# Layer 0 attention: DVE's copy and maximum stand ahead of the next pair's query piece in a step, not behind it

## The reference, cut to what matters

```python
q_lat = rmsnorm(hidden_states @ q_a_w, q_a_norm_w)
q = (q_lat @ q_b_w).reshape(b, s, H, QKD).transpose(0, 2, 1, 3)
...
q_pe = rope_interleaved(q_pe, pos)
scores = (jnp.einsum('bhqd,bhkd->bhqk', q_nope, k_nope) + jnp.einsum('bhqd,bhkd->bhqk', q_pe, k_pe)) * QKD ** (-0.5)
...
scores = jnp.where(mask[:, None], scores, -jnp.inf)
attn = jax.nn.softmax(scores, axis=-1)
out = jnp.einsum('bhqk,bhkd->bqhd', attn, v).reshape(b, s, H * VD)
```

## Time and profile before

| | |
|---|---|
| median of 3 runs | 1736.12 us (1732.72 to 1740.18) |
| the profiled execution | 1737.15 us, its span 1735.4 us |
| layer 0 attention in it | from about 520 to 1115 us |
| busy, share of the span | PE 94%, DVE 62%, ACT 49%, POOL 41% |
| mean granted clock of PE | 0.986 of full |

### The profile page before, as it was taken

One profiled execution on the slowest core, in us unless ns is written; L12 is line 12 of the kernel. 1 busy time (PEld: TensorE's weight loads), 2 busy tenths in 40 slices (PEclk: granted clock), 3 DMA queues, 4 the chain that ended last, 5 costly groups with the idle time before them and its releaser, 6 DMA issues. The chain is left out here.

```text
span 1735.4 us, 27207 instructions
## 1 busy us (share of the span) xinstructions
PE 1631.3 (94%) x8810; PEld 1220.1 (70%) x8810; DVE 1080.6 (62%) x2489; ACT 847.6 (49%) x1591; POOL 716.8 (41%) x740
## 2 busy tenths in 40 slices
PE   6899998999988999999999999899989999999998
PEld 5688887788776766776677777587755555568887
DVE  3556657999838767777777777435776776510222
ACT  3456555443326555555555555444245565653321
POOL 1212213444657656666556666376201111322221
PEclk9999999999999999999999999999989999999999
DMA  8522223221100000000000000373432332231111
GB/s 243 171 76 90 91 77 93 60 63 34 55 31 7 25 19 19 31 19 20 25 19 19 31 19 13 92 236 122 151 62 50 84 66 61 51 103 55 49 49 49
DMA packets 113020, 114.16 MB, mean 66 GB/s; under 512 B 39776, under 2 KB 72000, under 8 KB 112896
## 3 DMA queue, kind: packets, MB, share of 16 engines
q1 hardware_dynamic: 110592, 108.40, 21.9%
q10 hardware_dynamic: 2304, 4.20, 0.7%
HBM read 83.97 MB, written 28.44 MB: 65 GB/s over the span
## 5 line engine op out<-in xcount | busy, mean ns | idle before, releaser
L1463 ACT ACTIVATE a_p<-a_sm,a_nmax 128x640 f32<-128x640 f32 (+7 forms) x256 | 198.7, 778 | 142.6 <-DVE a_nmax L1424 140.9
L1506 POOL TENSOR_SCALAR a_p<-a_p,a_rinv 128x640 f32<-128x640 f32 (+7 forms) x256 | 191.9, 753 | 165.0 <-DVE a_rinv L1432 162.1
L1424 DVE CUSTOM_DVE_ANT_0 a_sm<-ps,maskb 128x640 f32<-128x640 f32 (+7 forms) x256 | 192.0, 750 | 98.4 <-PE ps L1368 96.5
L2360 DVE CUSTOM_DVE_ANT_0 ga_sm<-ps,strip 128x640 f32<-128x640 f32 (+1 forms) x224 | 163.1, 754 | 71.2 <-PE ps L2267 69.7
L2381 ACT ACTIVATE ga_pt<-ps 128x1024 f32<-128x1024 f32 (+1 forms) x192 | 147.9, 810 | 112.7 <-PE ps L2290 111.7
L1380 PE MATMUL ps<-ident,a_p 128*128 128x128 f32 x1152 | 172.4, 275 | 14.0 <-DVE a_pt L1439 13.8
L1380 PEld LDWEIGHTS ps<-ident,a_p 128*128 128x128 f32 x1152 | 135.3, 140 | 39.7 <-issue 16.9
L2421 POOL TENSOR_SCALAR_AFFINE_SELECT ga_pt<-ga_pt 128x512 f32<-128x512 f32 x64 | 40.7, 636 | 265.1 <-ACT ga_pt L2381 265.0
L1368 PE MATMUL ps<-kh,lq_qh 128*128 128x512 f32 (+4 forms) x384 | 128.8, 389 | 18.4 <-DVE a_nmax L1424 11.6
L940 DVE SCALAR_TENSOR_TENSOR idx<-ix_r,ix_sgc,idx 128x256 f32<-128x256 f32 (+6 forms) x105 | 90.7, 884 | 73.9 <-ACT ix_r L905 73.9
L1395 PE MATMUL ps<-a_pt,vst 128*64 128x512 f32 (+3 forms) x768 | 134.2, 492 | 1.9 <-DVE a_pt L1439 1.1
(11 more groups left out here) (313 smaller groups left out, 3979.2 us busy)
## 6 DMA issues: line engine op xcount, KB each, us to landing
idx<-ctx_d SPq DMA_DIRECT2D x32, 256.0 KB, 3.3
idx<-wvo_d SPq DMA_DIRECT2D x32, 256.0 KB, 3.8
ga_qst<-qkd SPq DMA_DIRECT2D x42, 128.0 KB, 4.2
f_wr<-in_L_ffn_w SPq DMA_DIRECT2D x18, 256.0 KB, 2.8
x<-in_L_attn_hidden_states SPq DMA_DIRECT2D x16, 256.0 KB, 4.3
op_wo<-in_L_attn_o_w SPq DMA_DIRECT2D x8, 512.0 KB, 5.0
ix_w<-in_L_attn_idx_wq_w SPq DMA_DIRECT2D x64, 64.0 KB, 1.9
ix_fo<-in_L_attn_o_w SPq DMA_DIRECT2D x8, 512.0 KB, 4.1
```

The lines of the kernel that those rows point to most:

```text
L1424: dve.tensor_tensor_reduce(out=in_row(sm[kind][:, 0:w], w), in0=in_banks(slots[kind], w), in1=in_row(maskb[:, MASK_OFF[t]:MASK_OFF[t + 1]] ...
L1463: act.activation(p[kind][:, v // 2 % 2, 0:w], sm[kind][:, 0:w], ACT.Exp, bias=nmax[:, v % 4:v % 4 + 1], scale=-1.0, accum_out=rsum[:, v % ...
L1506: pool.tensor_scalar(mine, mine, rinv[:, v % 4:v % 4 + 1], 1.0, ALU.mult, ALU.mult).then_inc(norm_done, 1)
L2360: dve.tensor_tensor_reduce(out=in_row(sm[kind][:, 0:w], w), in0=in_banks(slots[kind], w), in1=in_row(strip[:, S - w:], w), scale=-1.0, sca ...
```

## The change

In DVE's step, `dve_hook` moves from behind the inverse to the end. In steps 3, 5, 8 and 11 (and -5 and -3 of the lead-in), DVE so copies the transposed blocks of unit `u+2` and takes the maximum of unit `u+7` first and turns the piece of queries after that. In all other steps the hook is empty and nothing changes. The programs of the other engines, all semaphores and all their counts stay the same.

```diff
@@ -1442,11 +1442,11 @@
                 def step(i, u, left):
                     if there(u + 5, left):
                         inverse(i, u + 5)
-                    q["dve"](dve, i, u, left)
                     if there(u + 2, left):
                         keep(i, u + 2)
                     if there(u + 7, left):
                         maximum(i, u + 7)
+                    q["dve"](dve, i, u, left)
```

## The result

| | before | after |
|---|---|---|
| median | 1736.32 us (6 runs) | 1804.11 us (6 runs, 1801.61 to 1812.39) |
| ratio | | 1.0396, interval 1.0376 to 1.0415 |
| the profiled execution, span | 1735.4 us | 1801.5 us |
| mean granted clock of PE | 0.986 | 0.981 |

The forecast was 1794 us, with 1765 to 1812 around it. The page after, against the earlier trace rows; the instruction counts are the same.

The account below looks back on a forecast made before the run. PE was taken to bound the kernel, busy 94% of the span. Costs of 3.96 us in each of 14 pairs plus 2.7 in pair 0 sum to 58.1 us, giving 1794 us against the median, range 1765 to 1812.

Parts of the forecast that it names:

- First cost: Step 3: piece 0 waits behind unit 10's maximum, so PE's product for piece 1 gets its bank 1.45 us later.
- Second cost: Step 5: piece 1 waits behind unit 12's maximum, delaying POOL's low half; unit 16's scores 3.74 us later, including 1.45 from step 3.
- Steps 9 to 14: From unit 16's scores to step 14: DVE stalls go, POOL's queue takes their place, 0.22 us lost a pair.
- most of the 0.74 us a pair that PE waits for copies is gone: Sign of being right: PE's transposes mostly stop waiting for DVE's copies out of the transpose banks.
- The sum: 3.96 us a pair over pairs 1 to 14 (55.4), 2.7 in pair 0, lead-in 0: 58.1 us in all.
- The lead-in: Before pair 0: the 2.31 us stop goes but unit 8 waits for piece 3; taken as 0, bounds -2.3 and +1.
- The clock: PE's new stops of about 1.5 us each were taken to cost 0 beyond themselves, by the lead-in's 2.31 us stop.
- Rival (c): PE's clock also falls behind the new stops, 1 to 2 us a pair: 1815 us; chance 0.05.
- (a): Rival: PE waited for copies and maxima, and the pieces have slack; 18 us come back, 1718 us; chance 0.06.
- (b): Rival: one cost only; just the bank wait, 1758 us, or just the second cost, 1771 us; chance 0.12.
- (d): Rival: the effects cancel or DVE's order shows nowhere, 1733 to 1740 us; chance 0.05.
- The gain: At most all of PE's two DVE stalls, for copies and maxima: 1.21 us a pair, 18 us over 15 pairs.

Follow-up runs that it names:

- step3: Kernel before the change, with only step 3's query piece (piece 0) moved behind copy and maximum on DVE: 1762.2 us, ratio 1.014.
- step5: Kernel before the change, with only step 5's query piece (piece 1) moved behind copy and maximum on DVE: 1769.0 us, ratio 1.0185.

## Why the prediction was right, and where it was not

- **First cost, 1.45 us.** Measured 1.61, and 1.59 alone in step3. The mechanism is the one told. The term was short mainly by the hand-over to PE: DVE's piece ends at 1079.49 and the product starts at 1079.64, 0.15 in place of the 0.04 that I took from a hand-over in the other direction. The maximum took 0.05 more than the 0.95 allowed, up to the piece's start.
- **Second cost, 2.29 us** (3.74 less 1.45). Measured 2.21 to the scores of unit 16. The queue on POOL is as told: two normalisings in 1.58, between the add and the low half.
- **Steps 9 to 14, 0.22 us.** Measured 0.01 to unit 17's transposes and 0.06 behind them. The path is the one told: unit 18's maximum, piece 3, POOL's add, unit 17's normalising. It takes 10.26 in place of 10.47 because the stall of 0.35 that goes is worth 0.57 from start to start (scores of unit 16 to scores of unit 18: 4.40 before, 1092.22 to 1096.05 after). What was wrong is "most of the 0.74 us a pair that PE waits for copies is gone": it is 0.97 a pair (11.6 in 12). A copy behind piece 1 is 0.3 late in step 7 and one behind piece 3 is 0.68 late in step 13. I had only asked which copies come earlier by standing ahead of a piece, and not which come later behind it in the next step. They cost little here, since PE waits for POOL's queue right behind each.
- **The sum.** 3.96 forecast for a pair, 3.86 measured; 2.7 and 2.5 for pair 0; the period of 41.0 that would show it is 40.9. The lead-in ended 0.95 us later, inside its bounds: the stop of 2.31 us is down to 0.54, and smaller ones come in its place, the longest 0.89 us for piece 3's low half ahead of unit 8's scores, as told.
- **The clock, 0 in the sum.** This is the term that was mis-sized: the four falls in pairs 0 to 14 cost 6.4 us, most of the 10 us by which the median is over the forecast. The fall in pair 15 adds 2.6, and kernels without the new stops have that one too, so it is not put down to the change. The step that failed was to take the 2.31 us stop of the lead-in the earlier trace rows as showing that a shorter stop costs nothing beyond itself. (The same lead-in has one of 1.57 us, at 531.78, with the clock at full behind it as well.) That such a stop passed at full clock shows that it can, not that it must: the clock fell behind four of 30 stops of 1.64 to 1.78 us. Rival (c), in which it falls in each pair, named the mechanism and priced a fall at 1 to 2 us (measured 1.5 to 1.7), but gave it all pairs or none. The Trainium skill (TensorE: Matmul & The Clock Gate, section HAM oscillation) tells of a clock that drops at every burst where bursts of about 2 us are parted by waits of some 3 to 5 us. The stops here are shorter and most of them pass without a fall, so these runs agree with it in kind alone, and the forecast had applied it to stops shorter than those it is about.
- **The rivals.** (a) fails with the two new waits. (b) fails: step3 and step5 show each cost alone, +1.59 and +1.58. (d) fails by the ratio.
- **The gain.** I gave 18 us as its upper end and said that the pieces have no slack. The last kernel gets that gain, 20 us over 15 pairs, by a copy that moves ahead, a maximum that doesn't, and a piece 3 two steps later.

## What to carry to other kernels

Before work moves behind an instruction that waits, ask where what it waits for is issued: a maximum that needs the scores of the same step ties everything behind it to that step of PE, and a single bank and an in-order queue on a third engine pass it on. Move the half that waits for nothing, and take load out of the stretch where an engine is late; the first was worth 0.17 us a pair, the second 0.34 and both 1.35. Ask as well what stands behind the moved work in the next step. Where a forecast puts new stops like these on PE, put some falls of its clock into the sum: here a quarter of the stops of 1.64 to 1.78 us had one, at some 1.6 us each.

## What the runs showed of the hardware

- In pairs 0 to 14 PE's clock fell to its lower level only in the four kernels with stops of 1.64 to 1.78 us, behind 19 of 76 such stops (in two to eight of 15 pairs), for 1.5 to 1.7 us each. In pair 15 it fell in seven of eleven executions with stops of no more than 1.12 us.
- A stop in the profile can understate what its removal gives, since it is counted from a modelled end that the next matmul would have overlapped: moving POOL's add took 0.44 us off a pair where the stop before it was 0.27, and the stall of 0.35 ahead of unit 12's second transposes was worth 0.57.
- From the end of DVE's piece to the product that waits for its bank passed 0.14 to 0.15 us, 15 times in this kernel and 15 in step3; from the end of PE's scores to DVE's maximum 0.04 us.
